# Turning the quantised FFN activations: DMA transposes on ScalarE's queue in place of TensorE transposes and ScalarE copies

## The reference

```python
x = x + tanh(g_xattn[0]) * L0_xattn(layernorm(x), ctx, ...)   # 32 query heads, 8 key/value heads
x = x + tanh(g_ffn[0]) * L0_ffn(layernorm(x), w_gate, w_up, w_down)
x = x + tanh(g_xattn[1]) * L1_xattn(layernorm(x), ctx, ...)
x = x + tanh(g_ffn[1]) * L1_ffn(layernorm(x), ...)            # int4 weights, permuted input

def _mx_linear(x, w):
    return jnp.matmul(_mx_quant(x, 3), _mx_quant(w, 1).T)
gate, up = _mx_linear(x, w_gate), _mx_linear(x, w_up)         # 512 -> 1376
return _mx_linear(silu(gate) * up, w_down)                    # 1376 -> 512
```

## Time and profile before

| | |
|---|---|
| three runs | 1346.63 us median, 1345.92 to 1347.79 |
| the profiled execution, its own time | 1346.49 us |
| its span, first to last instruction | 1344.6 us |
| TensorE busy | 1336.9 us, 99% of the span |
| TensorE weight loads, VectorE, ScalarE, GpSimd busy | 1135.6, 960.4, 837.0, 635.2 us |
| granted TensorE clock | 1.000 |
| the steps with FFN work | about 540 to 776 us of the span |

### The profile page before, as it was taken

One profiled execution on the slowest core, in us unless ns is written; L12 is line 12 of the kernel. 1 busy time (PEld: TensorE's weight loads), 2 busy tenths in 40 slices (PEclk: granted clock), 3 DMA queues, 4 the chain that ended last, 5 costly groups with the idle time before them and its releaser, 6 DMA issues.

```text
span 1344.6 us, 25713 instructions
## 1 busy us (share of the span) xinstructions
PE 1336.9 (99%) x7841; PEld 1135.6 (84%) x7841; DVE 960.4 (71%) x1984; ACT 837.0 (62%) x3299; POOL 635.2 (47%) x682
## 2 busy tenths in 40 slices
PE   9999999999999999999999999999999999999999
PEld 7888888888888888777777788888888888888887
DVE  6878787887878798788888857766555555555656
ACT  6767676676767675556656556655666656565542
POOL 3456556564646575356767424432434333332232
PEclk9999999999999999999999999999999999999999
DMA  8011212102121210010100022001010100100001
GB/s 291 1 60 50 67 50 65 52 22 64 49 66 49 67 50 21 1 48 32 49 32 1 1 79 79 32 1 56 32 47 31 45 33 0 47 31 1 2 8 56
DMA packets 32957, 59.49 MB, mean 44 GB/s; under 512 B 2928, under 2 KB 24304, under 8 KB 28784
## 3 DMA queue, kind: packets, MB, share of 16 engines
q1 hardware_dynamic: 32592, 58.01, 13.0%
q10 hardware_dynamic: 288, 0.52, 0.1%
HBM read 56.43 MB, written 2.10 MB: 44 GB/s over the span
## 4 chain that ended last, share of the span: by engine, by line
PE 96%; DVE 1%; POOL 1%; issue 1%; DMA 0%; ACT 0%; SPq 0%; POOLq 0%; DVEq 0%; ACTq 0%
PE bank L1210 66%; PE bank L1202 9%; PE bank L1274 8%; PE bank L1301 7%; PE bank L1236 3%; PE bank L1395 1%; PE bank L1291 1%; PE bank L1407 1%; DMA w_raw<-in_wv 0%; DVE w_lo L823 0%; PE bank L1382 0%; POOL probs L560 0%; POOL rstd L523 0%; DVE probs L1046 0%; POOL f_s L513 0%
## 5 line engine op out<-in xcount | busy, mean ns | idle before, releaser
L494 POOL TENSOR_TENSOR w_lo<-w_raw,w_hi (+1 forms) x150 | 210.7, 1420 | 174.9 <-ACT w_hi L661 174.9
L694 ACT ACTIVATE squares<-bank 128x128 bf16<-128x128 f32 x512 | 134.4, 278 | 196.3 <-PE bank L1210 196.3
L1046 DVE SCALAR_TENSOR_TENSOR probs<-bank,mask_sb 128x512 f32<-128x512 f32 x127 | 87.6, 690 | 205.6 <-PE bank L1274 190.8
L642 ACT ACTIVATE probs<-probs,negmax 128x128 f32<-128x128 f32 x512 | 198.4, 392 | 7.0 <-DVE negmax L929 4.5
L519 POOL TENSOR_TENSOR meansq<-sumsq,scalars 128x5 f32<-128x5 f32 x128 | 28.1, 219 | 359.1 <-ACT squares L694 359.1
L523 POOL TENSOR_TENSOR rstd<-meansq,scalars 128x5 f32<-128x5 f32 x128 | 153.1, 1196 | 10.8 <-POOL meansq L519 1.1
L1210 PE MATMUL bank<-w_hi,oT_hi 128*128 (+1 forms) x512 | 151.1, 417 | 0.0
L1210 PE MATMUL bank<-w_hi,xT_hi 128*128 (+1 forms) x512 | 141.1, 396 | 0.0
L1210 PE MATMUL bank<-w_lo,oT_hi 128*128 (+1 forms) x512 | 138.1, 391 | 0.0
L1210 PE MATMUL bank<-w_hi,oT_lo 128*128 (+1 forms) x512 | 137.9, 391 | 0.0
L1210 PE MATMUL bank<-w_lo,xT_hi 128*128 (+1 forms) x512 | 137.6, 390 | 0.1
(11 more groups left out here) (143 smaller groups left out, 3058.7 us busy)
## 6 DMA issues: line engine op xcount, KB each, us to landing
w_raw<-in_wq SPq DMA_DIRECT2D x16, 1024.0 KB, 4.9
w_raw<-in_wo SPq DMA_DIRECT2D x16, 1024.0 KB, 4.8
fw_raw<-in_ffn_w SPq DMA_DIRECT2D x36, 192.0 KB, 2.3
w_raw<-in_wk SPq DMA_DIRECT2D x16, 256.0 KB, 5.3
w_raw<-in_wv SPq DMA_DIRECT2D x16, 256.0 KB, 5.4
x_sb<-in_x SPq DMA_DIRECT2D x7, 256.0 KB, 9.6
ctx_raw<-in_ctxT SPq DMA_DIRECT2D x7, 256.0 KB, 9.1
fw_raw<-in_ffn_w SPq DMA_DIRECT2D x7, 256.0 KB, 2.7
```

The source lines that it names most:

```text
L494: last = nc.gpsimd.tensor_tensor(lo, raw, hi.bitcast(FP32), ALU.subtract)
L642: last = nc.scalar.activation(probs[:, h * P:(h + 1) * P], probs[:, h * P:(h + 1) * P], ACT.Exp, bias=negmax[:, h:h + 1], accum_out=rowsum ...
L694: last = nc.scalar.activation(squares[:, h // 2, (b + 1) % 4, h % 2, :], q_bank(n, kind)[:, h * P:(h + 1) * P], ACT.Square, scale=SCALE, a ...
L1046: nc.vector.scalar_tensor_tensor(heads(probs[:, :]), heads(psSQ[:, :]), SCALE, mask_sb[:, :].unsqueeze(1).to_broadcast([P, REP, P]), ALU.m ...
```

## The change

The identity `ident_bf` and its two GpSimd operations at the start go, and so do all 15 TensorE transposes of a tile and ScalarE's four copies. ScalarE's queue issues four DMA transposes for a tile instead, from SBUF to SBUF: one of `f_xq` at the place of the old copy, one of chunk 0 before the squares of the queries of the down step (earlier than the old copy), and those of chunks 1 and 2 one behind the other at the place of the old copies. Each waits for `six_done` itself. The last one moves 384 columns of the slot, of which 352 are used. TensorE's down product waits for each chunk's own semaphore before the first row block of that chunk; VectorE's write into `f_iq` and `f_xq` waits for the DMA that reads the slot.

```diff
-        ident_bf = sb("ident_bf", [P, P], BF16)
-        psC_bf = psC[:, :].bitcast(BF16)
...
+            def hidden_turned(c, i):
+                first, tiles = CHUNKS[c][0] // P, (CHUNKS[c][1] + P - 1) // P
+                act.wait_ge(six_done, SIX[c, i] + 1)
+                wait(act, d_ps, i)
+                act.dma_start_transpose(f_iqT[:, first:first + tiles, :], f_iq[:, c % 2, 0:tiles * P]).then_inc(iT_sb[c], 16)
...
                 if t.gate is not None:
-                    act.wait_ge(fxT_ps, t.gate + 1)
+                    act.wait_ge(six_done, SIX["in", t.gate] + 1)
                     wait(act, gu_ps, len(CHUNKS) * t.gate)
-                    nc.scalar.activation(f_xqT[:, :, :], by_k(psC_bf[:, 0:D]), ACT.Copy).then_inc(fxT_sb, 1)
+                    act.dma_start_transpose(f_xqT[:, :, :], f_xq[:, :]).then_inc(fxT_sb, 16)
+                if t.down is not None:
+                    hidden_turned(0, t.down)
...
                     gate_tanh(2, t.down)
-                    act.wait_ge(i0_ps, t.down + 1)
-                    wait(act, d_ps, t.down)
-                    nc.scalar.activation(f_iqT[:, 0:4, :], by_k(psC_bf[:, 0:D]), ACT.Copy).then_inc(i0_sb, 1)
...
-                    act.wait_ge(ib_ps, t.down + 1)
-                    wait(act, d_ps, t.down)
-                    nc.scalar.activation(f_iqT[:, 4:10, :], by_k(psC_bf[:, 0:6 * P]), ACT.Copy)
-                    rows = ITILES[-1][1]
-                    nc.scalar.activation(f_iqT[0:rows, 10, :], psC_bf[0:rows, 6 * P:7 * P], ACT.Copy).then_inc(ib_sb, 1)
+                    hidden_turned(1, t.down)
+                    hidden_turned(2, t.down)
...
                 if t.down is not None:
                     gate_up(2, t.down)
-                    pe.wait_ge(six_done, SIX[0, t.down] + 1)
-                    transposes(f_iq[:, 0, :], psC_bf, ident_bf[:, :]).then_inc(i0_ps, 1)
...
-                    transposes(f_xq, psC_bf, ident_bf[:, :]).then_inc(fxT_ps, 1)
...
-                    for k in range(4, NT):
...
-                        last = nc.tensor.transpose(psC_bf[0:rows, (k - 4) * P:(k - 3) * P],
-                                                   f_iq[:, c % 2, at:at + rows], ident_bf[:, :])
-                    last.then_inc(ib_ps, 1)
...
                 if t.down is not None:
-                    pe.wait_ge(ib_sb, t.down + 1)
+                    wait(pe, d_acc, t.down)
                     for k, (r, rows) in enumerate(ITILES):
+                        if r in CHUNK_STARTS:
+                            pe.wait_ge(iT_sb[CHUNK_STARTS.index(r)], 16 * (t.down + 1))
                         col = (DOWN_BLOCK + KT * k) * P
```

More of the change, by code:

```diff
@@ L49 @@
 CHUNKS = [(0, 512), (512, 512), (1024, NI - 1024)]
+CHUNK_STARTS = [first for first, _ in CHUNKS]
 ITILES = [(s, min(P, NI - s)) for s in range(0, NI, P)]
@@ L282, in flamingo_kernel @@
         six_read, clipped, six_done = sem("six_read"), sem("clipped"), sem("six_done")
-        fxT_ps, fxT_sb, gate_ps, gu_ps, tanh_done, gated, up_used, i0_ps, i0_sb, ib_ps, ib_sb, d_ps, d_acc = (sem(n) for n in (
-            "fxT_ps", "fxT_sb", "gate_ps", "gu_ps", "tanh_done", "gated", "up_used", "i0_ps", "i0_sb", "ib_ps", "ib_sb", "d_ps", "d_acc"))
+        gate_ps, gu_ps, tanh_done, gated, up_used, d_ps, d_acc = (sem(n) for n in (
+            "gate_ps", "gu_ps", "tanh_done", "gated", "up_used", "d_ps", "d_acc"))
+        fxT_sb, iT_sb = sem("fxT_sb"), [sem(f"i{c}T_sb") for c in range(len(CHUNKS))]
         loaded_w4, loaded_bias, iota_done, nibbles, w4_scaled, w4_done, wp_ps, wp_hid, wp_lod, biased = (sem(n) for n in (
@@ L478, in _ @@
         def _(pool):
-            for t in (ident, ident_bf):
-                nc.gpsimd.memset(t[:, :], 0.0).then_inc(consts_bf, 1)
+            nc.gpsimd.memset(ident[:, :], 0.0).then_inc(consts_bf, 1)
             nc.gpsimd.memset(minus_half[:, :], -0.5).then_inc(consts_bf, 1)
             nc.gpsimd.memset(eps_sb[:, :], EPS).then_inc(consts_bf, 1)
[L483 to L486, removed]
+            pool.wait_ge(consts_bf, 3)
+            nc.gpsimd.affine_select(out=ident[:, :], in_=ident[:, :], compare_op=ALU.not_equal, fill=1.0,
+                                    base=0, pattern=[[-1, P]], channel_multiplier=1).then_inc(consts, 1)
             def split_lower(pieces):
@@ L897, in quantise6 @@
                 if c == "in":
-                    wait(dve, fxT_ps, i)
+                    wait(dve, fxT_sb, 16 * i)
                     dst = f_xq[:, :]
@@ L901, in quantise6 @@
                     if c < 2:
-                        wait(dve, ib_ps, i)
+                        wait(dve, iT_sb[2 - c], 16 * i)
                     else:
-                        dve.wait_ge(i0_ps, i + 1)
+                        dve.wait_ge(iT_sb[0], 16 * (i + 1))
                     dst = f_iq[:, c % 2, 0:width]
@@ L1363, in step @@
                 if t.gate is not None:
-                    pe.wait_ge(fxT_sb, t.gate + 1)
+                    if t.gate == 0:
+                        pe.wait_ge(wt_sb, QUANT_PIECES + 1)
+                    pe.wait_ge(fxT_sb, 16 * (t.gate + 1))
                     pe.wait_ge(xT_lod, BATCHES + max(t.gate - 1, 0))
@@ L1373, in step @@
                     output()
-                if t.down is not None:
-                    pe.wait_ge(six_done, SIX[2, t.down] + 1)
-                    pe.wait_ge(i0_sb, t.down + 1)
-                    for k in range(4, NT):
-                        r, rows = ITILES[k]
-                        c = 1 if k < 8 else 2
-                        at = r - CHUNKS[c][0]
-                        last = nc.tensor.transpose(psC_bf[0:rows, (k - 4) * P:(k - 3) * P],
-                                                   f_iq[:, c % 2, at:at + rows], ident_bf[:, :])
-                    last.then_inc(ib_ps, 1)
                 if has(n, 0):
@@ L1435, in keep_clock @@
                     nc.tensor.transpose(psSQ[:, 0:P], ident[:, :], ident[:, :])
-            pe.wait_ge(consts, 2)
+            pe.wait_ge(consts, 1)
             keep_clock(21)
```

## The result

The changed kernel takes **1352.83 us** (median of five runs, 1351.51 to 1353.81); the kernel before, run beside it, 1346.72 us (1345.92 to 1347.79, five runs). The profiled execution took 1352.83 us, its span is 1351.0 us, 6.4 us above that of before.

What follows compares the result with a forecast made beforehand. TensorE, 99% busy, was taken to bound the kernel. Gate and down terms less landing waits gave a gain between 0.26 and 2.08 us; the middle, 1.2, off 1346.49 gave 1345.3 us, range 1343.8 to 1360.

Steps and rivals of the forecast that it cites:

- rival 2: Tiles 2 to 4: transposes of chunk 2 and `f_xq` end only with weight loads, 8.5 us late, 1353.8 us; chance 0.08.
- L: Time until a DMA transpose has landed, taken as 2.6 us for every tile.
- a room of 3.6 us: Down step: time from chunk 2 being scaled to the ninth of eleven row blocks needing it, 3.6 us.
- The clock: FFN steps: short holes of 0.6 us don't lower TensorE's clock, so it was left out of the sum.
- Rival 3: Gate, then down products: landing above the room makes TensorE wait, from 3.1 us; 1360 us at 4 us; chance 0.22.
- The two room cases: Gate steps, tiles 2, 4, 5, 6: room 2.55 us if the issue waits for `w_hi`, 3.80 if the queue runs ahead.
- The gate steps: Four TensorE transposes fewer give 0.24 us in each of tiles 1 to 7, 1.68 us at best.
- Tile 0: Gate step: TensorE waits for GpSimd's `probs` anyway, so nothing is gained; the landing costs 0.16 us.
- The down steps: Eleven TensorE transposes fewer, but `values()` waits for `pT_lo`: gain 0.07 us a tile, 0.56 us in all.
- the prediction's signs: Signs of being right included `values()` in down steps waiting about 0.6 us for `pT_lo`.
- H: Down step: ScalarE held by issuing chunk 2's transpose, 0.45 us, covered by 1.65 us before `kT`.

Runs made afterwards that it cites:

- experiment 12: Changed kernel with wo loaded by two DMAs of 64 partitions each, rows of 8 KB: 1354.38 us, ratio 1.0052.
- experiment 6: Changed kernel with the two wo loads inside the FFN steps (tiles 2 and 4) held until chunk 2 is turned: 1346.34 us, ratio 0.9999.
- experiment 13: Changed kernel with wo loaded by two DMAs, first 128 KB, then 896 KB: 1345.96 us, ratio 0.9995.
- experiment 4: Changed kernel with the DMA transposes left out and only their semaphores raised, so the first FFN adds nothing: 1345.68 us, ratio 0.9993.
- experiment 14: Changed kernel with wo loaded by two DMAs, first 896 KB, then 128 KB: 1351.15 us, ratio 1.0038.
- experiment 1: Changed kernel with wo loaded by four DMAs with rows of 2 KB in place of 8 KB: 1346.59 us, ratio 1.0000.
- experiment 8: The changed kernel run again, unchanged, for a second trace: 1352.35 us, ratio 1.0048.

## Why the prediction was wrong

**The failed step** is the price and the chance of rival 2, "the weight loads get in the way". Its mechanism as written, a transpose that "ends only with the load", and its arithmetic, "2.1 us late, twice (tiles 2 and 4)", are what happened: 1.81 and 2.10 us of wait in one trace, 1.84 and 1.92 in the other. What put it at 0.08 was the sentence "both transposes are issued before the load". Being issued first does not protect a transpose: one that has not landed when the load's packets begin lands with the load's first DMA. Chunk 2's data starts at 632.51, the load's at 632.77, and in experiment 12 it did not even help that the data were through when the load began. In the sum the step is the one L for all tiles: chunk 2 was given 2.6 us of landing in a room of 3.6 us, so no wait at the down product, while in tiles 2 and 4 it took up to 5.7 us and TensorE lost 1.94 and 2.35 us (1.97 and 2.05). The same sentence was right for tile 3's `f_xqT`, which the rival also charged, with 4.3 us: its last packet is of 641.24, and wq is issued only at 641.87.

**The clock** was left "out of the sum" because holes of 0.6 us did not lower it. Holes of 2 us did: tile 5's gate step took 1.18 and 1.31 us more. That the rival's 1353.8 us lies so near the result is partly chance: its 4.3 us for tile 3 did not come, the clock's 1.2 us did.

**The landing** L was put at 2.6 us, from 1.7 and 5.4: 2.4 us in the median. That it came so near is partly luck. The row was read as "the only load on ScalarE's own queue", "with little beside it"; but `ctx_raw`, the other load on that queue, took 4.2 us, and both ran at the start, where the 16 DMA engines were 85% busy and more from 2 to 4 us. The estimate of 5.2 us from the Trainium skill, "VectorE: DVE Perf Modes", section "The three transpose paths" (1309 ns for a block, times four), is not borne out. The Trainium skill, "Advanced Engine Details and Errata", section "DMA Advanced Topics", has transposes as fast as other DMAs; the 2.4 us for 128 KB lie between the store of 128 KB, 1.7 us, and the load of 256 KB, 2.6 us, which does not speak against it. Rival 3, with its threshold of 3.1 us in every tile, did not come.

**The two room cases.** The queue runs ahead of its engine: chunk 1 is issued at 629.22, in the middle of `xT_hi` (628.90 to 629.50, timeline of tile 2 above). So the gate product never waited for a landing in tiles 1 to 7, the case for which 2.08 us were worked out, and not the middle, 1.2 us.

**The gate steps** nevertheless gained less than the 0.24 us a tile of that case: 0.24 in tiles 1 and 7 and behind a hole, but 0.06 to 0.11 in the others (0.01 in tile 3 of experiment 6). TensorE is 0.24 us ahead until the middle of `gate_up(1)` and waits there for VectorE's `f_q`. Tile 4 of the changed kernel, VectorE, TensorE's weight loads and GpSimd:

```profile
675.96 0.55 DVE L892 TENSOR_SCALAR blk_pow<-amax 128x16 uint32<-128x16 uint32 x1
676.42 0.68 DVE L893 SCALAR_TENSOR_TENSOR f_q<-bank,inv_pow 128x512 fp8e4<-128x512 f32 x1
...
677.15 0.55 PEld L1235 LDWEIGHTS bank<-wT,f_xqT 128*128 128x128 bf16 x4 [0.46 <-DVE f_q L893]
...
675.72 2.30 POOL L511 TENSOR_SCALAR qn<-x_sb,ln_mv,ln_rstd 128x512 f32<-128x512 f32 x1 [0.47 <-PE bank L1201]
```

and of the kernel before, VectorE and GpSimd:

```profile
672.50 0.18 DVE L893 TENSOR_SCALAR blk_pow<-amax 128x16 uint32<-128x16 uint32 x1
...
672.48 2.08 POOL L513 TENSOR_SCALAR qn<-x_sb,ln_mv,ln_rstd 128x512 f32<-128x512 f32 x1 [0.77 <-PE bank L1202]
```

GpSimd's `qn` waits for TensorE, so it comes 0.24 us sooner too. Before, it began together with `blk_pow`; now it begins 0.24 us ahead of it, and both take longer, `blk_pow` 0.55 us in place of 0.18 and `qn` 2.30 in place of 2.08. The later `f_q` is what TensorE waits for. In tiles 1 and 7 and behind a hole the two begin together again and `blk_pow` takes 0.18 to 0.20. Why both take longer side by side is not shown. The gate steps are a term that was too large: 0.95 us in place of 1.68 (experiment 13). Tile 0 lost 0.22 where 0.16 was said.

**The down steps** gained 0.03 to 0.05 us where 0.07 was forecast, tile 0's nothing, and tile 3's lost 0.08: 0.12 us in all in place of 0.56 (experiment 13), the other term that was too large. Where the rest of the 0.64 us went shows in tile 3's step, VectorE, TensorE and its weight loads (PEld) in the changed kernel:

```profile
660.98 0.68 DVE L933 TENSOR_TENSOR pT_lo<-bank,pT_hi 128x512 fp32r<-128x512 f32 x1
...
657.56 0.63 PE L1201 MATMUL bank<-ident,qn 128*128 128x128 f32 x4 [0.26 <-DVE bank L917]
...
661.12 0.65 PE L1201 MATMUL bank<-ident,qn 128*128 128x128 f32 x4
661.12 0.42 PEld L1201 LDWEIGHTS bank<-ident,qn 128*128 128x128 f32 x4 [0.42 <-DVE qn L941]
661.72 0.50 PE L1300 MATMUL bank<-pT_hi,v_hi 128*128 128x512 f32 x1
```

`values()` starts at 661.72, 0.06 us behind the end of `pT_lo`, where it was 0.12. The time of chunk 0's transposes turned into a wait of 0.26 us for VectorE's L917, seven times (1.8 us in the list of waits), and most of that of the seven others into a wait of its weight loads for VectorE's `qn`, which stands ahead of `pT_lo`: 0.42 us here, 0.3 in the other tiles from 1 on. So TensorE's idle time is there, but not, as the prediction's signs had it, some 0.6 us at `values()`: the longest wait for `pT_lo` is 0.2 us. In tile 3 alone a VectorE operation of `hidden(2)`'s quantisation (L887) took 0.64 us in place of 0.53, and `pT_lo` began 0.12 us later in the step. In all, the steps without a hole gave 0.97 and 0.92 us in the two traces, tile 0's loss taken off, beside the 1.2 us of the sum, which was the middle between 0.26 and 2.08 us. And with the meeting removed the kernel took 1345.96 and 1346.34 us (experiments 13 and 6), where the sum said 1345.3.

**H** was put at 0.45 us and is 1.2 us for each transpose. The room of 1.65 us covers it: `kT` starts 1.14 us behind the matmul that transposes the key in tile 2's down step (631.48), 1.06 before. In experiment 4, without any issue, it is 0.37 us, so the held queue does delay `kT`; but TensorE's steps gain the same there, 0.09 to 0.10 us in tiles 2 to 6 and 0.23 in tiles 1 and 7. H costs nothing.

## What to carry to other kernels

When a DMA is put on a critical path, list every load whose packets can begin before it has landed, whichever queue issues it and however early it was issued, and price it as landing with that load's first DMA. Where they must meet, hold the load back or let a small DMA go first; here that cost nothing that could be measured and gave back about 6 us. And before removing work from the busiest engine, read what the next instruction waits for: here even free turning was worth 1 us.

## What the runs showed of the hardware that was not expected

- A transpose whose data had all moved at 634.35 raised its semaphore only between 636.30 and 637.27, with the first DMA of a load on another queue. At tile 2, in nine of the ten traces with such a meeting, the last 4-byte packets of the two lie within 0.03 us of each other; with four DMAs by partitions they lie 0.7 us apart. At tile 4 it is seven of ten: the others are 0.1 us (four DMAs by partitions), 0.15 us (experiment 14) and 2.3 us apart (experiment 1, the instruction fetch).
- ScalarE's queue is held 1.2 us by a DMA transpose of 128x512 bf16 (shortest 1195 ns), where a plain one took 0.45 us.
- VectorE's `blk_pow` of 128x16 took 0.18 us when it began together with GpSimd's `qn`, and 0.55 us when `qn` had begun 0.24 us before it (2.3 us in place of 2.08 for `qn`).
- The clock fell to the level of 1.2 GHz for 3 to 4 us after TensorE had stood idle for 1.9 to 2.1 us. It fell after the second hole in all five traces with two holes of about 2 us (the second 1.92 to 2.11 us), after the first in one of them only (2.13 us, experiment 12; 1.73 to 2.04 in the others), and not after the single one of 2.44 us in experiment 1. It also fell at the start behind an idle of 1.95 to 2.17 us for the first weights, in three traces, that of the changed kernel among them (from 11.7 us); it cost nothing that shows there: from unit 0 to unit 1 that trace lost 0.36 us on the one of before, and the one of experiment 8, whose clock did not fall there, 0.38. And of the five runs of the changed kernel two (1351.51 and 1352.63 us) have a mean clock of 1.000: the fall does not come in every execution. What tells these apart stays open.
